# Exponentials of the local attention layers taken per head straight from PSUM, with the query's length as scale and the row maximum as bias

## The reference

```python
q, k, v = split(shift_tokens(x) @ Wqkv, 3)      # 128 -> 3 x 1024
q = l2norm(q) * qs;  k = l2norm(k) * ksc        # a length per token and head
q = q*cos*scale + rotate_half(q)*sin*scale      # rotary position
k = k*cos/scale + rotate_half(k)*sin/scale
sim  = 8 * q @ k2.T                             # a window of 32 queries sees 64 keys
attn = softmax(where(mask, -max, sim))
x = x + (attn @ v2) @ Wo
x = x + ffn(shift_tokens(x))                    # layer norm, 128 -> 2 x 341, gelu gate, 341 -> 128
```

## Time and profile before

| | us |
|---|---|
| median of 3 runs | 4878.06 (4871.51 to 4888.29) |
| the profiled execution | 4875.73 |
| its span (first to last instruction) | 4874.4 |
| stage d, first to last query projection | 1402 to 4747 |

### The profile page before, as it was taken

The page is one execution under the profiler, slowest core; times in us unless marked ns, Lnnn a source line. Parts: engine busy times, 40 slices in busy tenths (PEclk is TensorE's granted clock), DMA queues, the critical chain, the costliest instruction groups (busy, mean ns, idle before and its releaser), DMA issues.

```text
span 4874.4 us, 139104 instructions
## 1 busy us (share of the span) xinstructions
PE 4219.5 (87%) x57664; PEld 3041.7 (62%) x57664; DVE 3887.6 (80%) x6471; ACT 3235.4 (66%) x5034; POOL 3717.0 (76%) x2624
## 2 busy tenths in 40 slices
PE   7886566658868999999999999999999999999997
PEld 5664455546635666666666666666666666666665
DVE  4665999935557888888888888888888888888994
ACT  4664888844435677677776767666776676767775
POOL 1112888833358998899998989889998898988993
PEclk9998787889988999999999999999999999999999
DMA  2000000000001222222222222222222222222222
GB/s 60 2 2 1 1 1 1 1 26 2 2 1 42 52 51 59 57 53 54 54 58 55 56 52 51 64 55 57 50 60 59 55 53 51 60 53 56 51 57 55
DMA packets 120832, 198.72 MB, mean 41 GB/s; under 512 B 66896, under 2 KB 78224, under 8 KB 120080
## 3 DMA queue, kind: packets, MB, share of 16 engines
q1 hardware_dynamic: 120208, 189.82, 15.9%
HBM read 24.12 MB, written 2.10 MB: 5 GB/s over the span
## 4 chain that ended last, share of the span: by engine, by line
PE 54%; ACT 13%; DVE 11%; issue 8%; POOL 6%; DMA 6%; SPq 1%; DVEq 0%; ACTq 0%; POOLq 0%
PE ps L1306 8%; PE ps L1250 8%; PE ps L1251 7%; DMA arena<-arena 6%; PE ps L1259 5%; DVE arena L1489 3%; PE ps L1347 3%; PE ps L1358 2%; PE ps L1297 2%; PE ps L1341 2%; PE ps L1298 2%; ACT L1393 2%; PE ps L1278 2%; DVE arena L1482 2%; DVE arena L598 2%
## 5 line engine op out<-in xcount | busy, mean ns | idle before, releaser
L1582 POOL TENSOR_TENSOR arena<-arena 128x1024 f32<-128x1024 f32 x384 | 909.1, 2368 | 237.2 <-DVE arena L1482 236.9
L1577 POOL TENSOR_TENSOR arena<-arena 128x32 f32<-128x32 f32 x192 | 1045.4, 5445 | 0.1
L1481 DVE TENSOR_TENSOR arena<-ps,arena 128x1024 f32<-128x1024 f32 x384 | 470.2, 1224 | 314.9 <-ACT arena L1376 314.9
L1376 ACT ACTIVATE arena<-ps 128x1024 f32<-128x1024 f32 x384 | 393.0, 1024 | 375.1 <-PE ps L1251 370.5
L1600 POOL TENSOR_TENSOR arena<-arena 128x1536 f32<-128x1536 f32 x192 | 529.1, 2756 | 111.9 <-DVE arena L1515 111.9
L208 POOL TENSOR_SCALAR arena<-arena 128x2 f32<-128x2 f32 x256 | 72.7, 284 | 628.1 <-DVE arena L202 617.0
L1306 PE MATMUL ps<-arena 96*64 96x64 f32 x12288 | 424.4, 228 | 73.1 <-DMA arena<-arena 68.6
L1482 DVE TENSOR_TENSOR arena<-ps,arena 128x1024 f32<-128x1024 f32 x384 | 466.0, 1213 | 0.0
L1306 PEld LDWEIGHTS ps<-arena 96*64 96x64 f32 x12288 | 397.6, 140 | 105.0 <-issue 97.2
L1489 DVE TENSOR_REDUCE arena<-arena 128x32 f32<-128x2048 f32 x192 | 436.8, 2275 | 0.0
L1250 PE MATMUL ps<-arena 128*128 128x512 f32 x768 | 433.1, 646 | 0.9 <-ACT arena L1425 0.9
(11 more groups left out here) (251 smaller groups left out, 10039.7 us busy)
## 6 DMA issues: line engine op xcount, KB each, us to landing
arena<-arena SPq DMA_DIRECT2D x192, 384.0 KB, 4.4
arena<-arena SPq DMA_DIRECT2D x192, 256.0 KB, 3.7
arena<-arena SPq DMA_DIRECT2D x192, 128.0 KB, 2.3
arena<-in_dWqkv SPq DMA_DIRECT2D x18, 512.0 KB, 3.6
arena<-arena SPq DMA_DIRECT2D x96, 64.0 KB
arena<-arena SPq DMA_DIRECT2D x96, 63.5 KB
arena<-in_dWo SPq DMA_DIRECT2D x6, 512.0 KB, 4.9
arena<-in_x SPq DMA_DIRECT2D x4, 512.0 KB, 7.4
```

Source lines behind the costliest of these rows:

```text
L1376: act.activation(SQ[:, 1024 * g:1024 * g + 1024], ps(f"q{g}", n), ACT.Square).then_inc(*sq[g].up())
L1481: dve.tensor_tensor(o1, p.rearrange("p (h e) -> p h e", h=16), bc(cs, 1, 16), ALU.mult)
L1577: pool.tensor_tensor(ss[:, 0:32], ss[:, 32:64], mhalf32, ALU.pow).then_inc(*S.rs.up())
L1582: pool.tensor_tensor(a1[:, half], a1[:, half], T2[:, half], ALU.add).then_inc(*radd[g].up())
```

## The change

- The exponential is taken per head, straight from the scores in PSUM: 8 ACT instructions of 96 columns for each of `ex0`, `ex1` in place of one of 768. Scale is the query's 1/length (`SS`), bias is a new column of `SM`, and each gives its sum over the row (`accum_out`). The PSUM slot of `s0`, `s1` is thus freed by `ex0`, `ex1` (it was by the subtraction).
- DVE: the two subtractions and the sum over `P` go. New pieces `nb0`, `nb1` give −maximum x 1/length (128 x 8); `rc` keeps the reciprocal. `vn` moves from ACT to DVE.
- POOL: `nrm0` goes; `t0` waits for `radd0` alone. `rs` waits for the exponentials of three tiles earlier too.
- The squares and the rotary products are cut into halves of 512 columns: `sq0`, `sr0`, `sq1`, `sr1` on ACT, `rp0`, `ro0`, `rp1`, `ro1` on DVE; `rp` starts after `sq`, `ro` after `sr`, and the slot of `q0`, `q1` is freed by `ro` as before.
- All keys of `TILE` and `BATCH` are new, and so the order of every engine's pieces.

```diff
-    TILE = {"radd0": 0, "radd1": 114, "rs": 635, "ro0": 924, "ro1": 1055, "ssum": 1085, "halo": 1229, "nrm0": 1313,
-            "q0": 1338, "q1": 1606, "sq0": 1810, "sq1": 1922, "nrm1": 2759, "t0": 3300, "t1": 3445, "mx0": 3478,
-            "mx1": 3743, "qT": 3797, "s0": 3881, "kT": 3888, "s1": 4013, "pn": 4899, "ex0": 5254, "ex1": 5460,
-            "sum": 5842, "v": 6623, "p0": 6684, "p1": 6859, "vn": 7022, "vd": 7122, "xxa": 7210, "o": 7233,
-            "pT0": 7309, "pT1": 7427, "oT": 7658, "wo": 7722}
-    BATCH = {"sh": 189, "xs": 558, "fd": 10497, "fst": 12624, "frs": 13777, "fn": 16105, "ft": 16779, "fgm": 16933,
-             "fg": 16960, "fzT": 17348, "fge": 17533, "fa": 17592, "xxf": 17640, "fo": 17970}
+    TILE = {"radd0": 439, "rp0": 674, "radd1": 687, "ro0": 787, "q0": 1108, "rp1": 1239, "ro1": 1240, "sq0": 1339,
+            "q1": 1430, "rs": 1437, "ssum": 1448, "sr0": 1499, "sq1": 1614, "sr1": 1745, "halo": 1825, "nrm1": 2704,
+            "t0": 3024, "qT": 3292, "mx0": 3609, "nb0": 3641, "t1": 3967, "kT": 3991, "mx1": 4053, "s0": 4079,
+            "nb1": 4156, "ex0": 4404, "s1": 4592, "ex1": 4812, "rc": 4998, "pn": 5557, "vn": 6286, "vd": 6386,
+            "v": 6667, "p0": 7002, "p1": 7052, "pT0": 7126, "pT1": 7299, "o": 7681, "oT": 7836, "xxa": 7969,
+            "wo": 8341}
+    BATCH = {"sh": 0, "xs": 122, "fd": 9229, "fst": 11473, "frs": 13662, "fn": 15515, "fzT": 15840, "ft": 15915,
+             "fg": 16409, "fgm": 16423, "fge": 16512, "fa": 16689, "xxf": 16861, "fo": 17144}
...
-    freed = {... "s0": S.sub0, "s1": S.sub1, ...}
+    freed = {... "s0": S.ex0, "s1": S.ex1, ...}
...
             if piece in ("ex0", "ex1"):
                 g = int(piece[2])
-                P = PP[n % 3][:, 8 * g:8 * g + 8, :]
-                act.wait_ge(*sub[g].at(n + 1))
-                act.activation(P, P, ACT.Exp).then_inc(*ex[g].up())
+                P, ss, p = PP[n % 3], SS[n % 3], ps(f"s{g}", n)
+                if n >= 3:
+                    act.wait_ge(*p_ps[g].at(n - 2))
+                    act.wait_ge(*S.rc.at(n - 2))
+                act.wait_ge(*nb_[g].at(n + 1))
+                for x in range(8):
+                    h, at = 8 * g + 2 * (x % 4) + x // 4, 512 * (x // 4) + 96 * (x % 4)
+                    y = 8 * g + x
+                    i = act.activation(P[:, y, :], p[:, at:at + 96], ACT.Exp, bias=SM[n % 3][:, 3, y:y + 1], scale=ss[:, h:h + 1],
+                                       accum_out=SM[n % 3][:, 1, y:y + 1])
+                i.then_inc(*ex[g].up())
...
-            if piece in ("ro0", "ro1"):
+            if piece in ("rp0", "rp1", "ro0", "ro1"):
+                g, hf = int(piece[2]), "po".index(piece[1])
...
+                dve.wait_ge(*(sr if hf else sq)[g].at(n + 1))
+                dve.tensor_tensor(o1, p.rearrange("p (h e) -> p h e", h=8), bc(cs, 1, 8), ALU.mult)
...
                 dve.tensor_reduce(mg, pv, AX.X, ALU.max).then_inc(*S.step_dve.up())
+            if piece in ("nb0", "nb1"):
...
+                if n >= 3:
+                    dve.wait_ge(*ex[g].at(n - 2))
+                dve.wait_ge(*S.rs.at(n + 1))
                 dve.wait_ge(*S.step_dve.now())
-                dve.tensor_tensor(Pg, pv, bc(mg, 3, 96), ALU.subtract).then_inc(*sub[g].up())
-            if piece == "sum":
+                dve.scalar_tensor_tensor(nb..., mx..., -1.0, ss..., ALU.mult, ALU.mult).then_inc(*nb_[g].up())
+            if piece == "rc":
...
-                dve.tensor_reduce(sums, P, AX.X, ALU.add).then_inc(*S.step_dve.up())
...
+            if piece == "vn":
...
+                dve.tensor_copy(VN[n % 2], ps("v", n)).then_inc(*S.vn.up())
...
-            if piece == "nrm0":
...
-                pool.tensor_tensor(a3, a3, bc(ss[:, 0:16], 2, 64), ALU.mult).then_inc(*S.nrm_q.up())
```

More of the change, by code:

```diff
@@ L1179, in phase_d @@
         "step_dve step_pool sh_ps q_ps k_ps qt_ps kt_ps s0_ps s1_ps p0_ps p1_ps v_ps o_ps wo_ps ft_ps fg_ps fa_ps fo_ps",
-        "xs sq_q sq_k qT kT ex0 ex1 pT0 pT1 vn oT fn fzT fge en",
-        "ro_q ro_k ssum nrm_q nrm_k sub0 sub1 rc xxa fone fstat fgm xxf estat xe",
+        "xs sq_q sq_k sr_q sr_k qT kT ex0 ex1 pT0 pT1 vn oT fn fzT fge en",
+        "ro_q ro_k ssum nrm nb0 nb1 rc xxa fone fstat fgm xxf estat xe",
         "rs radd_q radd_k halo pn frs tab ers zeroed",
         "v0 v1 fs0 fs1 fs2 stored")
-    qk_ps, sq, ro, radd, nrm, t_ps = ((S.q_ps, S.k_ps), (S.sq_q, S.sq_k), (S.ro_q, S.ro_k), (S.radd_q, S.radd_k),
-                                      (S.nrm_q, S.nrm_k), (S.qt_ps, S.kt_ps))
-    s_ps, sub, ex, p_ps, pT, ld_qk = ((S.s0_ps, S.s1_ps), (S.sub0, S.sub1), (S.ex0, S.ex1), (S.p0_ps, S.p1_ps),
+    sr = (S.sr_q, S.sr_k)
+    qk_ps, sq, ro, radd, normed, t_ps = ((S.q_ps, S.k_ps), (S.sq_q, S.sq_k), (S.ro_q, S.ro_k), (S.radd_q, S.radd_k),
+                                         (S.radd_q, S.nrm), (S.qt_ps, S.kt_ps))
+    s_ps, nb_, ex, p_ps, pT, ld_qk = ((S.s0_ps, S.s1_ps), (S.nb0, S.nb1), (S.ex0, S.ex1), (S.p0_ps, S.p1_ps),
                                       (S.pT0, S.pT1), (L.ld_q, L.ld_k))
@@ L1201, in phase_d @@
     OT = [sb([128, 8, 128]) for _ in range(2)]
-    SM = [sb([128, 3, 16]) for _ in range(3)]
+    SM = [sb([128, 4, 16]) for _ in range(3)]
     FB = [(stats(C), sb([128, 2]), sb([128, 2, 128]), sb([128, 2, 128]), sb([128, 3, 256])) for _ in range(NF)]
-    TILE = {"radd0": 0, "radd1": 114, "rs": 635, "ro0": 924, "ro1": 1055, "ssum": 1085, "halo": 1229, "nrm0": 1313,
[4 rows of a table removed]
-    BATCH = {"sh": 189, "xs": 558, "fd": 10497, "fst": 12624, "frs": 13777, "fn": 16105, "ft": 16779, "fgm": 16933,
-             "fg": 16960, "fzT": 17348, "fge": 17533, "fa": 17592, "xxf": 17640, "fo": 17970}
+    TILE = {"radd0": 439, "rp0": 674, "radd1": 687, "ro0": 787, "q0": 1108, "rp1": 1239, "ro1": 1240, "sq0": 1339,
[5 rows of a table added]
+    BATCH = {"sh": 0, "xs": 122, "fd": 9229, "fst": 11473, "frs": 13662, "fn": 15515, "fzT": 15840, "ft": 15915,
+             "fg": 16409, "fgm": 16423, "fge": 16512, "fa": 16689, "xxf": 16861, "fo": 17144}
     LAYER = {"lqk": 32650, "lv": 37700, "lwo": 38900, "lw1": 47700, "lw2": 48200, "tab": 16000}
@@ L1227, in phase_d @@
             bufs.take((piece, l * NB + k))
-    freed = {"sh": S.xs, "q0": S.ro_q, "q1": S.ro_k, "t0": S.qT, "t1": S.kT, "s0": S.sub0, "s1": S.sub1, "p0": S.pT0,
+    freed = {"sh": S.xs, "q0": S.ro_q, "q1": S.ro_k, "t0": S.qT, "t1": S.kT, "s0": S.ex0, "s1": S.ex1, "p0": S.pT0,
              "p1": S.pT1, "v": S.vn, "o": S.oT, "wo": S.xxa, "ft": S.fzT, "fg": S.fge, "fa": S.fgm, "fo": S.xxf}
@@ L1253, in tile @@
                 g = int(piece[1])
-                pe.wait_ge(*nrm[g].at(n + 1))
+                pe.wait_ge(*normed[g].at(n + 1))
                 p, a1 = claim(piece, n), T1[n % 3][:, 1024 * g:1024 * g + 1024]
@@ L1375, in tile @@
                 act.wait_ge(*qk_ps[g].at(n + 1))
-                act.activation(SQ[:, 1024 * g:1024 * g + 1024], ps(f"q{g}", n), ACT.Square).then_inc(*sq[g].up())
+                act.activation(SQ[:, 1024 * g:1024 * g + 512], ps(f"q{g}", n)[:, 0:512], ACT.Square).then_inc(*sq[g].up())
+            if piece in ("sr0", "sr1"):
+                g = int(piece[2])
+                act.activation(SQ[:, 1024 * g + 512:1024 * g + 1024], ps(f"q{g}", n)[:, 512:1024], ACT.Square).then_inc(*sr[g].up())
             if piece == "qT":
@@ L1400, in tile @@
                                ps(f"p{g}", n)[0:96, :].rearrange("p (b h q) -> p b h q", b=2, h=8), ACT.Copy).then_inc(*pT[g].up())
[L1401 to L1407, removed]
             if piece == "oT":
@@ L1465, in tile @@
             n = l * NT + k
-            a1, ss, P = T1[n % 3], SS[n % 3], PP[n % 3]
-            mx, sums, rc = [SM[n % 3][:, i, :] for i in range(3)]
-            if piece in ("ro0", "ro1"):
[L1469 to L1476, removed]
-                cs, sn = tabs[l % 2][:, k % 2, 2 * g, :], tabs[l % 2][:, k % 2, 2 * g + 1, :]
[L1478 to L1483, removed]
+            a1, ss = T1[n % 3], SS[n % 3]
@@ new lines, in tile @@
+            mx, sums, rc, nb = [SM[n % 3][:, i, :] for i in range(4)]
+            if piece in ("rp0", "rp1", "ro0", "ro1"):
+                g, hf = int(piece[2]), "po".index(piece[1])
+                if hf == 0:
+                    if k == 0:
+                        dve.wait_ge(*S.tab.at(l + 1))
+                    if n >= 3:
+                        dve.wait_ge(*t_ps[g].at(n - 2))
+                    if n:
+                        dve.wait_ge(*radd[g].at(n))
+                at = 1024 * g + 512 * hf
+                p = ps(f"q{g}", n)[:, 512 * hf:512 * hf + 512]
+                cs, sn = tabs[l % 2][:, k % 2, 2 * g, :], tabs[l % 2][:, k % 2, 2 * g + 1, :]
+                o1 = a1[:, at:at + 512].rearrange("p (h e) -> p h e", h=8)
+                o2 = T2[:, at:at + 512].rearrange("p (h u e) -> p h u e", h=8, u=2)
+                dve.wait_ge(*(sr if hf else sq)[g].at(n + 1))
```

(34 more changed lines are left out.)

3 lines of the change are left out of this document (removed).

## The result

The changed kernel takes 5712.3 us (median of 4 runs, 5704.15 to 5719.91) against 4882.3 us: 1.170 of the time before, 95% interval 1.168 to 1.173. The forecast was slower, 5018 us, in a range of 4865 to 5125. The direction was right; the size, +830 us against +142, was not.

A forecast was written before the change was run, and what follows sets the result against it. It took a closed loop of PE and ACT through the exponentials as the bound: four groups (13.68) plus the ways made 36.66 us a pair against 35.18, +142 us over 96 pairs, so 5018 us, range 4865 to 5125.

The forecast's parts named there:

- A head at 0.415 us: On ACT, one head's exponential of 96 columns: 0.323 us plus 0.09 for its accumulator read; 8 heads a group.
- The loop of four groups of exponentials, 36.66 us a pair: Closed loop of PE and ACT through each pair's exponentials: four groups at 3.42 us plus the ways between, +1.48 a pair.
- the four ways: Paths between successive exponential groups: 4.47 us odd `ex0` to `ex1`, 5.76 even, 6.13 and 6.62 from `ex1` to next `ex0`.
- the one from the even `ex1` to the odd `ex0`: Path through key transposes, `p0`, `p1`, scores `s0`, projection `q0` and a half square: 6.13 us.
- fill and drain as before within 10 us: Start and end of the stage, outside the steady loop: claimed unchanged within 10 us.
- Level: `rp1`, `ro1` end as `o` ends.: VectorE's second rotary halves beside the loop: claimed to finish just as PE finishes piece `o`.
- two tiny `nb`: New VectorE instructions between maximum and exponentials: claimed between 0.1 and 0.25 us, taken as 0.2 each.
- VectorE at 27.3 us a pair is off the path: VectorE's work, net 1.6 us a tile less, 27.3 a pair: claimed off the path except `nb`.
- PE's work of 33.2 us a pair: PE's own work in the steady stretch, the 35.18 us period less 1.99 of waits: claimed unchanged.

The follow-up runs named there:

- Products twice: The changed kernel with the 32 products of piece `o` computed a second time on TensorE; 5519.8 us, 1.130 of the kernel before.

## Why the prediction was wrong

Against the forecast's own steps:

- *A head at 0.415 us* was right: the starts are 3504.55 − 3504.14 = 0.41 apart, and the read costs 0.085 to 0.09.
- *The loop of four groups of exponentials, 36.66 us a pair*, was right in mechanism and size: once `nb1` is free of POOL, one round takes 36.30, the mean period with the changes of layer is 37.08, and the time 5020.5, against 5018. Of the four ways three are within 0.04 of the forecast, and the one from the even `ex1` to the odd `ex0` is 0.44 shorter. That the two times are so close is partly luck: by the period alone it would be (37.08 − 35.18) x 96 = 182 us over the kernel before, and it is 143. Some 27 us of the difference lie at the start of the stage, where the first batch is done at 1657.4 us and not at 1684.9; the prediction had put fill and drain as before within 10 us. Taking the reads away (−2.71) and lengthening the way to `ex0` (+1.07) moved the period as the loop says.
- *Level: `rp1`, `ro1` end as `o` ends.* True without the stall, where PE waits for them 0.5 us in 2000; with it they are 2.5 us late.
- ***DVE ... two tiny `nb` ... between 0.1 and the 0.25 of the reciprocal; I take 0.2.*** This is the step that failed: a price of 0.2 us for each `nb`, and with it the premise that VectorE at 27.3 us a pair is off the path. `nb0` is 0.17, but `nb1` 2.64 in the mean and about 2.75 in most tiles. The price was bounded by an instruction of like size, without asking what else uses the path that its operands come by. The trace of before had a sign of it that was passed over: its clamp, one and the same instruction of 32 columns from SBUF, takes 235 ns at least and 2441 at most, and in all 192 tiles it runs beside POOL's addition `radd` (L1582). The reciprocal, of one operand, is 252 to 257 ns always; it was the wrong neighbour.
- *PE's work of 33.2 us a pair, which the change leaves as it is.* Wrong as a second consequence: with stalls of 2.5 us, not 0.9, the clock falls and the same matmuls take longer, 36.2 us a pair (1619.97/44.8).

The clamp of the kernel before, with minimum, median and maximum in ns:

```profile
L1491 DVE TENSOR_SCALAR arena<-arena x192: 235/504/2441, 1414.2 to 4752.9; 128x32 f32<-128x32 f32 x192
```

The account of the 44.68 us, by PE's busy and idle time in the two steady stretches: 37.08 with a short `nb`, of which PE is busy 32.8 and idle 4.3; with the long one it is busy 36.2, 3.4 more for the same matmuls at the lower clock, and idle 8.5, 4.2 more. The waits for the rotary products alone are 4.9, so that the other waits are 0.7 shorter. "Products twice" gives back 2.1 of the 3.4; whether the rest is the clock's or the price of the added products no run divides.

The rival that would have told it was not among the prediction's. The Trainium skill has it, in *SBUF — State Buffer*, "SBUF: two separate sides": the read and write port pair that VectorE and GpSimd share is an exclusive lock for a whole instruction, and a VectorE operation with two SBUF inputs, against a GpSimd operation that reads SBUF, or one in a two-port mode, asks for it. The runs agree for `nb1` beside `pn` (2.75 us with two SBUF operands, 0.17 with one). The clamp, with one operand, was held up as well; whether it ran in such a mode no run shows.

The runs differ from that rule in one place, and there they decide: beside POOL's power (`rs`, 5.4 us, two SBUF operands of 32 columns) VectorE instructions with two SBUF operands were not held up. `nb0` lies wholly within it in 190 of the 192 tiles of the changed kernel and never takes more than 0.17 us, and the multiplication of the keys in the kernel before (L1496, two SBUF operands, 1024 columns) lies wholly within it in 190 of 192 tiles too and takes 1212 to 1217 ns in all. Why the power leaves the way free stays open.

## What to carry to other kernels

When a tiny vector instruction is added to a latency path, look at where its operands lie and at what POOL does at that moment, before its size: one operand in PSUM turned 2.75 us into 0.17, and took some 690 us off the changed kernel. A chain that passes through many small activations is priced by their start-to-start distance, pointers and accumulator reads included; that distance and a walk round the slots of PSUM gave the period within 1.2% (36.66 against 37.08 us), once nothing else stood in the way. A sum that another engine takes is cheaper than 32 accumulator reads in the loop (4931 against 5020 us), and at a place of its queue where that engine is idle it is cheaper again (4781).

## What the hardware showed that I had not expected

A VectorE instruction of 8 columns with both operands in SBUF lasts until POOL's multiplication or addition beside it ends (2.75 us for 0.17), but not until the end of POOL's power (0.17); a clamp of 32 columns with one operand lasts until the end of POOL's multiplication too (1.83 for 0.18). The reductions, the reciprocal and the products with one operand in PSUM kept their durations within 0.07 us. A stall of TensorE of 2.5 us was followed by 4 us at a mean granted clock of 0.57; with stalls of 0.7 to 1.1 us only, the clock stayed at 0.99 in the steady stretch.
